# Storing the transposed normalised rows as fp16 halves in a cross-attention and mixture-of-experts kernel

## The reference

```python
x = x + xattn(layernorm(x), ctx, ctx, mask, Wq, bq, Wk, bk, Wv, bv, Wo, bo, 16)
n = layernorm(x).reshape(4096, 256)
def geglu(h): a, g = split(h, 2); return a * gelu(g)
ys = geglu(n @ Ws1 + bs1) @ Ws2 + bs2               # shared network, hidden width 512
logits = (n @ Wr + br) / 1.5                        # router, 12 experts
w = softmax of the two largest logits, zero elsewhere
yr = sum over e of w[e] * (geglu(n @ We1[e] + be1[e]) @ We2[e] + be2[e])
x = x + ys + yr
```

## Time and profile before

| | us |
|---|---|
| median of 3 runs | 1051.22 (1050.86 to 1053.73) |
| the profiled execution, its own time | 1056.09 |
| its span | 1054.4 |
| PE busy in the span | 942.1 (89%) |
| DVE busy | 713.2 (68%) |
| ACT busy | 567.7 (54%) |
| attention, slots 0 to 7 | to about 398 |
| tail with four early blocks | 398 to 458 |
| twelve shared blocks | 463 to 587 |
| experts | 587 to 1054 |

### The profile page before, as it was taken

The page is one execution under the profiler, slowest core; times in us unless marked ns, Lnnn a source line. Parts: engine busy times, 40 slices in busy tenths (PEclk is TensorE's granted clock), DMA queues, the critical chain, the costliest instruction groups (busy, mean ns, idle before and its releaser), DMA issues.

```text
span 1054.4 us, 26810 instructions
## 1 busy us (share of the span) xinstructions
PE 942.1 (89%) x7515; PEld 692.1 (66%) x7515; DVE 713.2 (68%) x1842; ACT 567.7 (54%) x1276; POOL 376.4 (36%) x537
## 2 busy tenths in 40 slices
PE   5578899989998887979998899999799999999996
PEld 3233444445453345768777689888688888998885
DVE  5776778878887634747766656776557677667753
ACT  3136555655655574324533656766446666667653
POOL 5300212545436262133320344445224543434342
PEclk9779999999999999989998989999999999999998
DMA  5552325263452141245664553555225445535232
GB/s 157 133 107 69 106 65 115 71 181 106 121 152 84 32 153 61 62 155 170 208 229 153 163 133 47 138 142 137 36 41 132 123 66 138 132 48 147 44 53 42
DMA packets 107927, 117.34 MB, mean 111 GB/s; under 512 B 20396, under 2 KB 99960, under 8 KB 107648
## 3 DMA queue, kind: packets, MB, share of 16 engines
q1 hardware_dynamic: 87168, 67.97, 23.8%
q0 software_dynamic: 20064, 47.20, 18.2%
q10 hardware_dynamic: 560, 0.53, 0.1%
HBM read 73.91 MB, written 38.87 MB: 107 GB/s over the span
## 4 chain that ended last, share of the span: by engine, by line
PE 40%; DMA 5%; issue 5%; DVE 3%; ACT 1%; SPq 1%; DVEq 1%; ACTq 0%; another core or an unknown queue 0%; POOL 0%; POOLq 0%
PE ff_psH L2312 24%; PE ff_psY L2339 13%; DMA ff_xrow<-expert_in 2%; DMA out_dram<-ff_x 2%; PE ff_psX L2266 2%; DVE ff_actf L2565 1%; PE ff_psH L2281 1%; DMA expert_in<-ff_zeros 1%; PE ff_psY L2296 1%; DVE ff_actl L2558 1%; DMA ff_x<-out_dram 0%; ACT ff_gel L2406 0%; SPq L1979 0%; ACT ff_acth L2401 0%; DVE ff_ysb L2641 0%
## 5 line engine op out<-in xcount | busy, mean ns | idle before, releaser
L2312 PE MATMUL ff_psH<-xh,ff_wx 128*128 128x256 f16 (+1 forms) x1776 | 270.8, 264 | 16.0 <-issue 10.6
L2312 PE MATMUL ff_psH<-xl,ff_wx 128*128 128x256 f16 (+1 forms) x888 | 218.7, 264 | 0.0
L1126 DVE TENSOR_REDUCE fast_negm<-fast_psS 128x2 f32<-128x512 f32 x256 | 168.2, 685 | 70.4 <-PE fast_psS L514 67.5
L886 ACT ACTIVATE fast_PT<-fast_psT 128x512 f32<-128x512 f32 x256 | 147.3, 596 | 104.6 <-PE fast_psT L546 102.0
L2247 POOL DMA_INDIRECT out_dram<-ff_ysc,ff_trow x78 | 124.7, 1599 | 195.4 <-ACT ff_ysc L2454 180.1
L2312 PEld LDWEIGHTS ff_psH<-xh,ff_wx 128*128 128x128 f16 x1776 | 167.6, 99 | 37.9 <-issue 14.8
L2565 DVE SCALAR_TENSOR_TENSOR ff_actf<-ff_psH,ff_b1T,ff_gel 128x256 f32<-128x256 f32 (+1 forms) x234 | 106.0, 454 | 101.9 <-ACT ff_gel L2406 97.3
L2406 ACT ACTIVATE ff_gel<-ff_psH,ff_b1T 128x256 f32<-128x256 f32 (+1 forms) x234 | 105.1, 450 | 83.2 <-PE ff_psH L2312 63.7
L2339 PE MATMUL ff_psY<-ff_wx,ff_acth 128*128 128x256 f16 x792 | 132.4, 273 | 0.8 <-DVE ff_actl L2558 0.7
L2401 ACT ACTIVATE ff_acth<-ff_actf 128x256 f16<-128x256 f32 (+1 forms) x282 | 110.6, 392 | 41.3 <-DVE ff_actf L2565 39.7
L514 PE MATMUL fast_psS<-fast_Kz,fast_Qs 128*128 128x512 f16 x256 | 100.4, 398 | 33.4 <-DVE fast_negm L1126 22.7
(11 more groups left out here) (276 smaller groups left out, 1683.4 us busy)
## 6 DMA issues: line engine op xcount, KB each, us to landing
ff_st<-in_L_ffn_We_dram POOLq DMA_DIRECT2D x12, 1536.0 KB
ff_xrow<-expert_in SPq DMA_DIRECT2D x41, 256.0 KB
ff_st<-in_L_ffn_We_dram POOLq DMA_DIRECT2D x12, 768.0 KB
fast_Qs<-qstk SPq DMA_DIRECT2D x48, 128.0 KB
fast_xbuf<-in_x_dram SPq DMA_DIRECT2D x8, 512.0 KB, 5.3
...
```

Of the source, the lines that this page charges most:

```text
L886: nc.scalar.activation(PT[:, n % NPT, :], psT[n % 2][:], ACT.Exp).then_inc(sem["exp_done"], 1)
L1126: nc.vector.tensor_reduce(negm[:, two(b), t, 2 * p:2 * p + 2], src, AX.X, ALU.max, negate=True).then_inc(sem["max_done"], 1)
L2312: mm = nc.tensor.matmul(psH[j % stage.banks][:, (half + 1) * NB - rows:(half + 1) * NB], a[:, dt, lo:lo + P], x[:, dt, NB - rows:], start= ...
```

## The change

Attention now makes the halves once and stores them.

- `set_x2T` on ACT writes `x2h`, fp16, in place of the fp32 `x2T`, and waits until the halves of the batch before are stored. DVE gets `x2_low(b, dt)`, two subtractions of 128x512 for a batch, in part 3 of the slot. The second transposes of x2 take bank 2 in place of bank 0 in the slots.
- `router` multiplies the halves, 24 fp16 matmuls of 12 columns in place of 8 fp32 products, and moves from the head of part 3 into part 4; `c_T(b+2)` moves behind `weigh(b, 1)`. Wr is split once, times 16, by two DVE instructions ahead of slot 0, which PE waits for; `logits` divides by 16 and moves behind two maxima.
- SP gets `save_x2(b-2)`, two stores of 256 KB into the new DRAM tensor `rows_T`, between `stack_q` and `write_k`, and in the tail for the last batch. In slot 7 the loads of the first two early blocks' halves come ahead of the loads of Ws1 and Ws2.
- The early blocks, and the twelve others, load their halves from `rows_T` into one of two buffers `x16` (256 KB, in pieces of 512 B). They transpose, copy and subtract nothing. The load of a block waits until the hidden products of the block before the last, which read the same buffer, are done. The experts' blocks still transpose and split.

The diff, cut to what carries this:

```diff
-MISC = dict(oX1=2, mT=0, xT0=1, xT1=0, Q0=1, Q1=2, x2T0=0, x2T1=0, oX2=1, R=0, oX3=2, V=1, cT=0, K=0, onT0=1, onT1=2, O0=1,
+MISC = dict(oX1=2, mT=0, xT0=1, xT1=0, Q0=1, Q1=2, x2T0=0, x2T1=2, oX2=1, R=0, oX3=2, V=1, cT=0, K=0, onT0=1, onT1=2, O0=1,
...
+        def save_x2(b):
+            until_sp("x2_low", of("x2_low", b, DT))
+            for part, tile in enumerate((x2h, x2l)):
+                sp.dma_start(scratch["x2"][bass.ds(b, 1), :, part * DT:(part + 1) * DT].rearrange("o p t q -> p (o t) q"),
+                             tile[:]).then_inc(sem["x2_saved"], 16)
             if b == B - 1:
+                early_blocks.load_x(sp, 0)
+                early_blocks.load_x(sp, 1)
                 until_sp("st_mm", of("st_mm", B - 2, 0))
                 sp.dma_start(raw_s[0], io["Ws1"].rearrange("(t p) f -> p t f", p=P)).then_inc(small, 16)
...
                 stack_q(b + 2)
+            if real(b - 2):
+                save_x2(b - 2)
+            if real(b + 2):
                 write_k(b + 2, 0)
...
         def router(b):
-            until(pe, "x2_set", of("x2_set", b, 2))
+            until(pe, "x2_low", of("x2_low", b, 2))
             ps = misc("R", b, "rt_link")
+            terms = [(x2h, "Wrh"), (x2h, "Wrl"), (x2l, "Wrh")]
             for t in range(QT):
-                mm = product(ps[:, t * E:(t + 1) * E], lambda dt: x2T[:, dt, t * P:(t + 1) * P], w_cols("Wr", 0, E))
+                for dt in range(DT):
+                    for i, (x, w) in enumerate(terms):
+                        mm = nc.tensor.matmul(ps[:, t * E:(t + 1) * E], x[:, dt, t * P:(t + 1) * P], keep[w][:, dt, :],
+                                              start=(dt == 0 and i == 0), stop=(dt == DT - 1 and i == 2))
...
         def set_x2T(b, dt):
             until(act, "r_mm", of("r_mm", b, 0))
+            until(act, "x2_saved", of("x2_saved", b, 0))
             until(act, "x2T_mm", of("x2T_mm", b, dt + 1))
-            copy_T("x2T", x2T, b, dt, "x2_set")
+            copy_T("x2T", x2h, b, dt, "x2_set")
...
+        def x2_low(b, dt):
+            until(dve, "x2_set", of("x2_set", b, dt + 1))
+            nc.vector.tensor_tensor(x2l[:, dt, :], psM[bank_at(f"x2T{dt}", b)][:], x2h[:, dt, :], ALU.subtract)\
+                .then_inc(sem["x2_low"], 1)
...
             slot(-1)
             dve.wait_ge(small, 16 * 4)
+            nc.vector.tensor_scalar(keep["Wrh"][:], keep["Wr"][:], WR_SCALE, None, ALU.mult).then_inc(wr_link, 1)
+            dve.wait_ge(wr_link, 1)
+            nc.vector.scalar_tensor_tensor(keep["Wrl"][:], keep["Wr"][:], WR_SCALE, keep["Wrh"][:], ALU.mult, ALU.subtract)\
+                .then_inc(wr_set, 1)
...
-    def rows_T(self, pe, m):
...
+    def load_x(self, sp, m):
+        if m >= 2:
+            sp.wait_ge(self.sem["h_mm"], (m - 1 + self.done) * SH_PAIRS)
+        sp.dma_start(self.x[m % 2][:].rearrange("p s t n -> p (s t) n"),
+                     self.stored_x[m // 2, :, :, m % 2 * NB:(m % 2 + 1) * NB]).then_inc(self.sem[f"x_in{m % 2}"], 16)
...
-        def load_shared(m, u):
-            until(shared, "xT_mm", of(shared, "xT_mm", m - 1))
-            sp.dma_start(xrow[:, u], keep["xn2"][:, bass.ds((m + EARLY) * NBT, NBT), 0:D])\
+        def load_shared(two, u):
+            until(shared, "h_mm", of(shared, "h_mm", two * 2 + u - 1))
+            rows = scratch["x2"][bass.ds(two + EARLY // 2, 1), :, :, u * NB:(u + 1) * NB]
+            sp.dma_start(x16[u][:].rearrange("p s t n -> p (s t) n"), rows.rearrange("o p s n -> p (o s) n"))\
                 .then_inc(shared.sem["odd_loaded" if u else "even_loaded"], 16)
...
         def shared_block(m, u, more=None, between=None):
-            ffn(shared, m, s1, s2, more or (shared, m + 1, 1 - u), between=between)
+            shared.until(pe, "odd_loaded" if u else "even_loaded", (m - (2 + u)) * 8 + 16)
+            ffn(shared, m, s1, s2, x16[u], more, between=between)
```

More of the change, by code:

```diff
@@ L703, in slot @@
             step()
+            if real(b - 2):
+                router(b - 2)
+            step()
+            weigh(b, 1)
             if real(b + 2):
                 c_T(b + 2, 0)
-            step()
-            weigh(b, 1)
             rest()
@@ L1737, in _ @@
     def _(sp):
-        blocks.load_rows(sp, 0)
-        blocks.load_rows(sp, 1)
+        for m in range(2):
+            blocks.load_x(sp, m)
+            blocks.load_rows(sp, m)
         for m in range(EARLY):
+            blocks.load_x(sp, m + 2)
             blocks.store_rows(sp, m)
@@ L1744, in _ @@
         blocks.all_stored(sp)
+        blocks.all_loaded(sp)
     @block.tensor
@@ L1804, in keep_tensors @@
         keep["s2" + x] = sb("s2" + x, [P, SH_PAIRS, D], FP16)
-    keep["xh"], keep["xl"] = (sb(n, [P, DT, NB], FP16) for n in ("xh", "xl"))
+    keep["x16"] = [sb(f"x16_{u}", [P, 2, DT, NB], FP16) for u in range(2)]
+    keep["Wrh"], keep["Wrl"] = (sb(n, [P, DT, E], FP16) for n in ("Wrh", "Wrl"))
     keep["bs1T"] = sb("bs1T", [P, 2 * SH_PAIRS], FP32)
@@ L1837 @@
 NSH = N // NB - EARLY
+WR_SCALE = 16.0
 LEFT_FROM = 2
@@ L1936, in feed_forward @@
     b2 = sb("b2", [P, E, D], FP32)
-    xrow = sb("xrow", [P, 2, NBT, D], FP32)
-    xh, xl = keep["xh"], keep["xl"]
+    xrow = sb("xrow", [P, NBT, D], FP32)
+    x16 = keep["x16"]
+    xh, xl = (x16[0][:, part] for part in range(2))
     gel = sb("gel", [P, 2, NB], FP32)
@@ L2303, in over_few, with ffn @@
             of_pair(EX_PAIRS - 1, False, True)
-        def ffn(stage, m, wa, wb, more, rows=NB, between=None):
+        def ffn(stage, m, wa, wb, x, more, rows=NB, between=None):
             n = stage.pairs
+            xh, xl = (x[:, part] for part in range(2))
             def hidden(j, half, terms, begins, ends):
@@ L2323, in ffn @@
                     hidden(j, 0, of_low, False, True)
-                for half in range(0 if j else 1, 2):
+                for half in range(1 if j == 0 and halves_come else 0, 2):
                     mm = hidden(j, half, [of_high[0], of_low[0], of_high[1]], True, True)
@@ L2328, in ffn @@
                     between()
-            if more:
-                row_transposes(*more)
+            if more is not None:
+                row_transposes(more)
             stage.until(pe, "y_ready", of(stage, "y_ready", m))
```

177 lines of the change are left out of this document (81 added, 96 removed).

## The result

| | before | changed |
|---|---|---|
| median, us | 1051.72 (1050.86 to 1053.73, 4 runs) | 1065.64 (1064.24 to 1068.36, 4 runs) |
| ratio of the times | | 1.0116 (95%: 1.0088 to 1.0144) |
| profiled execution: span, mean clock | 1054.4, 0.973 | 1064.1, 0.969 |

The forecast was 1056.5, from 1041.5 to 1063.0: the direction was right, and the size was under half of what came.

What follows compares the result with a forecast made beforehand. PE nearly fills a slot, with PE and DVE waiting on each other in part 3 and stacks through SP closing it. Attention +11.4, tail −4.7, shared blocks −2.1, pieces +0.7 gave +5.3: median 1056.5 us, range 1041.5 to 1063.

Steps and rivals of the forecast that it cites:

- The router on PE: Router alone on PE: 24 fp16 matmuls take 0.62 us in place of 1.71, saving 1.09 us a batch.
- weight loads count: Rival, router on PE: each 12-column matmul costs 107 ns, +1.94 us in each of 8 batches, 1072 us; chance 0.05.
- Slots 2 to 4, the engines: Attention slots 2 to 4: bank, subtractions, moved router and K wait lengthen each slot by about 2.1 us.
- the delay at the score of part 3: Part 3 of a slot: later bank +0.35, subtractions on DVE +1.2, less 0.53 idle time, make PE's score +1.0 us later.
- the K wait: Part 4 of a slot: with less work between, K waits for ACT's copy of the context, +0.48 us.
- Slot 7: Last attention slot: two loads of halves delay Ws1 and Ws2 by 2.1 us, less 0.6 hidden PE work: +1.5.
- SP and the stacks: SP's queue in slots 2 to 4: stores ahead of the K writes delay the K stack, +0.2 to +0.7 us each.
- the stacks decide: Rival, slots 2 to 5: K stack 3.9 us late, 2.1 covered, so 5.6 us more, 1062 us; chance 0.15.
- Tail: After attention: fewer transposes, copies and subtractions and a shorter router save 4.7 us in all.
- Shared blocks: Shared blocks: dropped transposes and subtractions save 2.1 us; loading halves from DRAM in 512 B pieces adds 0.7.
- Start: Ahead of slot 0: splitting Wr with two small DVE instructions holds the start by 0.3 us.
- The rival on the faster side: Rival, attention slots: subtractions fit into DVE's gaps, each slot keeps the router's 1.09 us, total −10.0, 1041 us; chance 0.26.

Runs made afterwards that it cites:

- before_ws: Kernel before the change, with the loads of Ws1 and Ws2 put first in SP's slot 7: 1047.84 us, ratio 0.9988.
- change_again: The changed kernel, unaltered, run and profiled a second time: 1060.54 us, ratio 1.0114 to the kernel before.
- loads_later: Changed kernel with the first two early blocks' loads of halves moved behind Ws1 and Ws2 in SP's slot 7: 1069.82 us, ratio 1.0126.
- stores_behind: Changed kernel with the two stores of the halves moved behind the K stack in each slot: 1066.41 us, ratio 1.0131.
- ws_first: Changed kernel with Ws1 and Ws2 loaded ahead of the other loads and stores of SP's slot 7: 1061.20 us, ratio 1.0061.
- rb_stores: Changed kernel with the router at the end of part 3 and the stores of the halves behind the K stack: 1063.98 us, ratio 1.0112.
- combos: Changed kernel, router ending part 3, Ws1 and Ws2 first in slot 7, stores between K writes and K stack; without or with Wr's split behind slot 0: 1049.23, 1047.98 us.
- sub_small: Changed kernel with DVE's two subtractions cut from 512 to 8 columns, the rest of the low halves left zero: 1062.41 us, one run.
- router_back: Changed kernel with the router at the end of part 3, context transposes and logits at their places of before: 1076.62 us, ratio 1.0206.
- base: The kernel before the change, unaltered, profiled a second time: 1058.33 us in the profiled execution.
- first pair: First profiles of the kernel before and the changed kernel, compared stage by stage: spans 1054.4 and 1064.1 us.
- combo_mid_wr: Changed kernel, router ending part 3, Ws1 and Ws2 first in slot 7, stores between K writes and K stack, Wr split behind slot 0: 1047.98 us, ratio 0.9996.
- second pair: Profiles from one chip of before_ws and change_again, compared stage by stage: spans 1047.0 and 1059.0 us.

## Why the prediction was wrong, by its own steps

- **The router on PE**: right. 0.62 forecast, 0.61 measured; the rows of the rank product were the right ones, and the rule of the Trainium skill ("TensorE: Matmul & The Clock Gate", "Back-to-back issue gap", some 81 ns a pair), which is for 128 columns, does not describe these 12-column products at 25 ns. The rival that weight loads count falls with it.
- **Slots 2 to 4, the engines**: right in mechanism and nearly in size. Forecast +2.1; measured +2.4, +2.0 and +1.5 where the clock holds (the 45.0 of slot 4 before held the 1.15 of waiting for the stack; against the 43.9 of before_ws it is +2.6). By steps in slot 3: the delay at the score of part 3 is 211.60 − 205.64 − (191.15 − 186.28) = +1.09, forecast +1.0; the K wait is 0.41, forecast 0.48. Not forecast: 0.84 us before the output transposes at 223.16, for the V bias on DVE; the cover that I named was thinner, as the text allowed.
- **The clock**: the first step that failed. The sum priced what PE waits by the length of the wait, with all durations taken at the clock of 1.00 that the earlier trace rows show, so a loss of clock stood in it at nothing, without a reason. In the five profiles with the slot order of the change (changed, change_again, loads_later, stores_behind, ws_first) PE waited 1.75 us in each of slots 2 to 4; in 8 of these 15 the clock fell and the slot took over 48 us. With 1.15 us in the same place (rb_stores, both combos) it fell in 0 of 9, with 1.47 (sub_small) in 0 of 3; with 2.9 to 3.3 at the slot's head (router_back) in 3 of 3. At 2.1 to 2.8 us each (the 49.9 of ws_first has 0.8 of waiting at the slot's head as well), eight losses in five profiles are about 4 us an execution. That the clock fell, and what it cost, is shown by the same slots of the same program with and without it. That the length of the wait brings it on is not: the seven waits of 1.5 to 2.5 us at other places left it alone. And the clock by itself does not leave the range: 5.3 + 4 = 9.3, where the range's end stood 11.8 above the median. The next step is needed too.
- **Slot 7**: the second step that failed, with the mechanism right and the size wrong. "Two loads … ahead of them now: +2.1, less 0.6 of PE work that this hides": the loads cost 3.1 (7.7 to 4.6 us on ACT in loads_later). And the stage is bound by the weights, so the time gained ahead of them is given back as waiting: they landed 2.9 us later in the slot than before, ACT came to them 2.5 us sooner, and its wait grew by the sum, 2.25 to 7.70. The row of ACT waiting 2.25 us said that a transfer paces this stage. The clock came on top: it stood at 0.50 for 12.6 us of the stage in the changed kernel, for 3.4 us before. From slot 7 to the first early product the pairs of the table have +4.0 and +2.0 for a forecast of −0.5; the second would be between −0.4 and +1.4 against the 47.5 to 49.3 of the kernel without before_ws's edit.
- **SP and the stacks**: forecast 0.2 to 0.7 a slot; in the change no first score of slots 2 to 5 waited over 0.4 us, less than the 1.15 of before, and 0 to 1.8 in the profiles of the same order. The text also expected the first score of slot 4 to wait about 2; it did not wait. The engines were late by about as much as the stack. The rival "the stacks decide" was false for the change and true for the next version: router_back.
- **Tail**: −2.4, −3.5 for a forecast of −2.7 after the first hidden product. Ahead of it −2.0 was forecast; from the x2 transposes of the tail to the hidden product PE took 425.99 − 421.32 = 4.67 for 408.25 − 402.49 = 5.76, 1.1 less, with the clock at 0.50 for all of it (before, for 3.4). **Shared blocks**: −0.6 to −0.9 on one chip each (before_ws and change_again; base, 119.4, and the mean 118.5 of the changed kernels beside it), −4.7 in the first pair; forecast −1.4. The 512 B pieces showed no price. Since the stage differs by 5 us between the profiles of two chips, the first pair alone would have misled.
- **Start**: +1.0 to +1.7 for +0.3; combo_mid_wr suggests half of it to be the split, not more than suggests.
- **The rival on the faster side** (the subtractions find gaps) had 0.26 and fell: PE waits for them. The point that it named, the wait at 205.64, was the right place.

Together: forecast +5.3; the second pair, of one chip, has 1059.0 − 1047.0 = +12.0, which is 6.7 more. Of this the two losses of clock in slots 2 and 4 are 4.6, and slot 7 to the first early product is 2.5 (+2.0 for −0.5). The rest cancels: the start to slot 1 is 1.7 above the forecast, slots 2 to 4 without the losses 0.9 below it (7.0 for 7.9), the tail 0.8 below.

What stays open: why the same wait of 1.75 us costs the clock in one slot and not in the next, and whether the wait or what stands around it brings the loss on. The combos keep the change's savings (against before_ws, 4.6 and 4.9 us in slot 7 to the first early product, 4.1 behind it), but slots 2 to 5 are 6.8 and 5.4 us longer, at a clock of 1.00, and that takes the most of it back. How this divides between the subtractions on DVE and the stacks was not measured in this order; the subtractions on another engine were not tried.
